# Attention keys and values stored as high and low parts by the phases that make them, and inverse sums spread by a broadcasting load

## The reference, cut to what matters

```python
q = rms_norm((x @ wq)...)      # 16 query heads of 128
k = rms_norm((x @ wk)...)      # 4 key/value heads of 128, 100 keys of x itself
v = x @ wv
k_ctx, v_ctx = rms_norm(h_ctx_kv @ wk_ctx), h_ctx_kv @ wv_ctx     # 722 keys of the context
q, k = rotary(q), rotary(k)
k_full, v_full = concat([k_ctx, k]), concat([v_ctx, v])           # 822 keys per batch
probs = softmax(q @ k_full.T * scale + mask)      # the mask is causal over the last 100 keys
out = (probs @ v_full) @ wo
```

## Time and profile before

| | |
|---|---|
| Median of 3 runs | 2796.28 us (2796.06 to 2798.22) |
| Profiled execution, its own time | 2798.06 us |
| Span of the profiled execution | 2796.0 us |
| Mean granted TensorE clock | 0.994 of full speed |
| PE busy | 2751.0 us, 98% of the span |
| DVE busy | 1586.5 us, 57% |
| ACT busy | 1104.9 us, 40% |
| Moved by DMA | 203.43 MB, 73 GB/s |
| Attention, 1445 to 1850 us: PE, DVE, ACT busy | 399.62, 345.32, 311.50 us of 405.00 |

### The profile page before, as it was taken

How to read it: one execution, slowest core, us unless ns; L and a number is a source line. 1 busy time by engine, 2 the same in 40 slices (tenths; PEclk the granted TensorE clock), 3 DMA queues, 4 the chain that set the end, 5 groups by cost and what they waited for, 6 DMA issues and landing times.

```text
span 2796.0 us, 39798 instructions
## 1 busy us (share of the span) xinstructions
PE 2751.0 (98%) x15494; PEld 2506.0 (90%) x15494; DVE 1586.5 (57%) x2106; ACT 1104.9 (40%) x1718; POOL 28.8 (1%) x45
## 2 busy tenths in 40 slices
PE   8999999999999999999999999999999999999997
PEld 7888889888888888898878888889999999998997
DVE  3223322344544454557778888854984573672767
ACT  3333322332323222334457777742542241341432
POOL 0000000000000000000000000000000000000000
PEclk9999999999999999999999999999999999999999
DMA  5222233221111111204122222212211121121222
GB/s 181 85 85 85 90 99 99 89 72 46 60 45 60 45 60 46 74 32 93 60 66 67 69 70 68 71 37 90 91 61 63 58 76 63 67 71 57 76 76 107
DMA packets 88137, 203.43 MB, mean 73 GB/s; under 512 B 9476, under 2 KB 64260, under 8 KB 73832
## 3 DMA queue, kind: packets, MB, share of 16 engines
q1 hardware_dynamic: 88040, 202.09, 21.7%
HBM read 171.86 MB, written 30.21 MB: 72 GB/s over the span
## 4 chain that ended last, share of the span: by engine, by line
PE 95%; DVE 3%; ACT 1%; issue 0%; DMA 0%; DVEq 0%; POOL 0%; SPq 0%; ACTq 0%
PE PS L128 8%; PE PS L130 8%; PE PS L129 8%; PE PS L2011 5%; PE PS L2009 5%; PE PS L2013 5%; PE PS L1533 5%; PE PS L434 3%; PE PS L435 3%; PE PS L436 3%; PE PS L409 3%; PE PS L410 3%; PE PS L411 3%; PE PS L1546 3%; PE PS L2046 3%; PE PS L2045 2%
## 5 line engine op out<-in xcount | busy, mean ns | idle before, releaser
L128 PE MATMUL PS<-XH,WH 128*128 128x512 f32 (+1 forms) x1216 | 424.5, 349 | 0.5 <-DVE t_ROOM L2281 0.5
L130 PE MATMUL PS<-XH,WL 128*128 128x512 f32 (+1 forms) x1216 | 419.7, 345 | 0.0
L129 PE MATMUL PS<-XL,WH 128*128 128x512 f32 (+1 forms) x1088 | 373.6, 343 | 0.0
L88 ACT ACTIVATE WH<-RAW 128x1024 fp32r<-128x1024 f32 x106 | 112.2, 1059 | 461.5 <-PE PS L130 329.6
L94 DVE TENSOR_TENSOR WL<-RAW,WH 128x1024 fp32r<-128x1024 f32 x106 | 129.6, 1223 | 244.8 <-ACT WH L88 244.2
L130 PEld LDWEIGHTS PS<-XH,WL 128*128 128x128 f32 x1216 | 228.8, 188 | 25.7
L128 PEld LDWEIGHTS PS<-XH,WH 128*128 128x128 f32 x1216 | 228.7, 188 | 24.9 <-ACT G L764 1.4
L129 PEld LDWEIGHTS PS<-XL,WH 128*128 128x128 f32 x1088 | 204.5, 188 | 23.0
L2137 ACT ACTIVATE WH<-RAW 128x512 fp32r<-128x512 f32 x180 | 113.5, 631 | 226.4 <-PE PS L2013 120.7
L409 PE MATMUL PS<-CH,KWH 128*128 128x338 f32 (+1 forms) x512 | 167.9, 328 | 12.9 <-DVE CL L385 12.9
L2370 DVE TENSOR_TENSOR WL<-RAW,WH 128x512 fp32r<-128x512 f32 x196 | 134.6, 687 | 60.5 <-ACT WH L2137 57.1
(11 more groups left out here) (316 smaller groups left out, 6577.8 us busy)
## 6 DMA issues: line engine op xcount, KB each, us to landing
RAW<-weights_dram SPq DMA_DIRECT2D x111, 1024.0 KB, 4.8
a_KRAW<-keys_scratch SPq DMA_DIRECT2D x32, 411.0 KB, 3.1
a_VRAW<-values_scratch SPq DMA_DIRECT2D x32, 384.0 KB
R<-context_dram SPq DMA_DIRECT2D x8, 1352.0 KB, 6.9
R<-context_dram SPq DMA_DIRECT2D x7, 1536.0 KB, 7.0
values_scratch<-VS SPq DMA_DIRECT2D x40, 256.0 KB
keys_scratch<-KS SPq DMA_DIRECT2D x8, 768.0 KB, 6.3
keys_scratch<-KS SPq DMA_DIRECT2D x8, 676.0 KB, 5.9
```

Source lines behind the costliest of these rows:

```text
L128: pe.matmul(out, wh, xh[:, k, cols], start=(k == 0), stop=False)
L129: pe.matmul(out, wh, xl[:, k, cols], start=False, stop=False)
L130: mm = pe.matmul(out, wl, xh[:, k, cols], start=False, stop=(k == KT - 1))
```

## The change

- The context phase writes the keys as a high part (ACT, `key_hi`) and a low part (DVE, `key_low`) into `KS`, one copy for both halves, and the values as a high part (ACT, `value_hi`) and a low part (DVE, a subtraction in place of the copy) into two tiles, the second of which lies in slot 0 of `RAW`. `kscr` and `vscr` have both parts, so each store becomes two.
- For that reason the weight stream of the retention phase waits until all value stores have landed.
- The heads phase does the same for the 100 keys and values of `x`. The first two values get their high parts (`value_hi`) on ACT after the loop over the kept values, the others and the keys in turns 0 and 1. The parts of the keys lie in parts of `QX` that the values or later heads use, so ACT waits before `key_hi(2)` until all 16 value stores have landed, and DVE waits in turn 1, head 0, before `finish`, until the four stores of keys 0 and 1 have landed.
- The attention phase loads the parts straight into the tiles that PE reads; the two ACT and the two DVE instructions are gone. Four small ACT instructions clear the padding once.
- The inverse sums are stored from `INV` to 1600 bytes of DRAM, and then loaded to all 128 partitions by one broadcasting load. The diagonal on POOL, the float32 matmul on PE and the copy on ACT are gone. The order in `SPREAD` is token, head in place of head, token.

```diff
@@ context
-        KS = sb("KS", [P, 2, KV_N, CA])
+        KS = sb("KS", [P, 2, KV_N, CA], F32R)
-        VS = sb("VS", [P, 3, KV_N * HD])
+        VS = [sb("VS", [P, 3, KV_N * HD], F32R)[:],
+              c.RAW[:, 0, 0:3 * KV_N * HD].bitcast(F32R).rearrange("p (t n) -> p t n", t=3)]
 store(b, e):
-                sp.wait_ge(k_out, 4 * (2 * b + e) + 4 + 4)
+                sp.wait_ge(k_lo, 4 * (2 * b + e) + 4 + 2)
+                for part in range(2):
+                    ... kscr[ds(b, 1), :, :, part, offset[e]:offset[e] + w] <- KS[:, part, :, 0:w]
                 sp.wait_ge(v_out, 6 * b + 3 * e + 3 + 2)
                 for t in range(3):
+                    for part in range(2):
+                        ... vscr[ds(b, 1), :, 0:rows, part, 3 * e + t, :] <- VS[part][0:rows, t, :]
 scalar, body:
+                    def key_hi(h):
+                        act.wait_ge(k_out, 8 * b + (n0 + h + 5))
+                        if h == 0:
+                            act.wait_ge(k_stored, 64 * b + (32 * e + 16))
+                        act.activation(KS[:, 0, h, 0:w], RS[:, h % 2, 0:w], ACT.Copy).then_inc(k_hi, 1)
+                    def value_hi(t):
+                        act.wait_ge(v_raw, 6 * b + (n + 1))
+                        if t == 0:
+                            act.wait_ge(v_stored, 192 * b + (96 * e + 16))
+                        act.activation(VS[0][0:rows, t, :], c.PS[0:rows, 4 + n % 2, :],
+                                       ACT.Copy).then_inc(v_hi, 1)
                     for h in range(KV_N):
+                        if h == 2:
+                            value_hi(0)
                         ...
-                        act.wait_ge(k_out, 8 * b + (n0 + h + 3))
+                        act.wait_ge(k_lo, 8 * b + (n0 + h + 1))
                         rsqrt_from(...)
+                        if h == 1:
+                            key_hi(0); key_hi(1); value_hi(1)
+                    key_hi(2); key_hi(3); value_hi(2)
 vector, body:
-                        dve.tensor_copy(VS[0:rows, t, :], ...).then_inc(v_out, 1)
+                        dve.wait_ge(v_hi, 6 * b + (n + 1))
+                        dve.tensor_tensor(VS[1][0:rows, t, :], c.PS[...], VS[0]..., ALU.subtract)
                     key_out(0)
                     key_out(1)
                     x_low(range(4, 6))
+                    key_low(0)
+                    key_low(1)
                     value_out(1)
                     x_low(range(6, 8))
                     key_out(2)
                     key_out(3)
+                    key_low(2)
+                    key_low(3)
                     value_out(2)
@@ retention, sync
             sp.dma_start(DECAY[:], c.decay).then_inc(c.const_in, 16)
             sp.dma_start(GNW[:], c.gnw).then_inc(c.const_in, 16)
+            sp.wait_ge(before.v_stored, 16 + 192 * B)
             weight_stream(c, sp, U_RET // 2 + 2, 2 * RH)
@@ heads
 sync:
             for v in range(KV_N):
                 sp.wait_ge(v_copied, v + 1)
+                for part in range(2):
                     for lo, hi, chunk, row in (...):
                         ... vscr[:, v, row:row + hi - lo, part, chunk, :] <- VT[part][lo:hi, v]
+            store_key(0)     # waits for k_lo, then two DMAs of 128 partitions
+            store_key(1)
             weight_stream(c, sp, U_V // 2 + 6, 1)
-            for v in range(KV_N): (store key v)
+            store_key(2)
+            store_key(3)
             weight_stream(c, sp, U_V // 2 + 8, 3)
 scalar:
             act.activation(ONE[:], c.ONES_HD[:], ACT.Copy)
+            value_hi(0)
+            value_hi(1)
+            def key_hi(v):
+                act.wait_ge(out, 2 + v + 1)
+                if v == 2:
+                    act.wait_ge(v_stored, 16 * V_STORES)
+                act.activation(key_parts(v)[0], key_raw(v), ACT.Copy).then_inc(k_hi, 1)
 scalar, turn, after SQH:
+                    if first and j < 2:  value_hi(j + 2)
+                    if first and j >= 2: key_hi(j - 2)
+                    if i is 1 and j < 2: key_hi(j + 2)
                     root(...)
 vector:
             copy_value(0)          # now waits for value_hi(0) and subtracts
             split_lo(c, dve, U_V + 4)
             copy_value(1)
             split_lo(c, dve, U_V + 5)
 vector, turn, after square_lo:
+                    if first and j < 2:  copy_value(j + 2)
+                    if first and j >= 2: key_low(j - 2)
+                    if i is 1 and j < 2:
+                        key_low(j + 2)
+                        if j == 0:
+                            dve.wait_ge(k_stored[0], 64)
                     finish(...)
+            after turn 1: dve.wait_ge(v_stored, 256); dve.wait_ge(k_stored[1], 64)
-            before turn 3: dve.wait_ge(stored, 16 * KV_STORES)
@@ attention
 sync, for each stage:
+                    sp.wait_ge(inverted, 4 * b + (v + 1))
+                    sp.dma_start(c.iscr, INV[:, v % 2, :]).then_inc(inverse_out, 16)
                     load_keys(next but one)      # now two DMAs, high and low
+                    sp.wait_ge(inverse_out, 64 * b + (16 * v + 16))
+                    sp.wait_ge(o_out, 4 * b + (v + 1))
+                    sp.dma_start(SPREAD[:], c.iscr.rearrange("(a t) g -> a (t g)", a=1)
+                             .broadcast_to([P, GT])).then_inc(spread, 16)
                     load_values(next)            # now four DMAs
 tensor:
-                    spread_inverse(b, v)         # between scores 1 of the next head and turn 2
 scalar:
-            keys_hi, values_hi, spread_out
 vector:
-            keys_lo, values_lo
 gpsimd:
-            diagonal(b, v)
```

More of the change, by code:

```diff
@@ new lines, in sync @@
+            store_key(2)
+            store_key(3)
+            weight_stream(c, sp, U_V // 2 + 8, 3)
+            sp.wait_ge(v_stored, 16 * V_STORES)
+            sp.wait_ge(k_stored[0], 64)
+            sp.wait_ge(k_stored[1], 64)
+            sp.wait_ge(before.k_stored, 16 + 64 * B)
+            sp.wait_ge(before.v_stored, 16 + 192 * B)
+            for part in range(2):
+                sp.dma_start(c.KHL0[:, part, 0:KEYS].bitcast(F32),
+                             c.kscr[0, 0, :, part, :]).then_inc(c.k_in, 16)
@@ L1278, in turn @@
                     act.activation(SQH[:], SQ[:], ACT.Copy).then_inc(sq_hi, 1)
+                    if first and j < 2:
+                        value_hi(j + 2)
+                    if first and j >= 2:
+                        key_hi(j - 2)
+                    if i is 1 and j < 2:
+                        key_hi(j + 2)
                     if final:
@@ L1284, in scalar @@
             turn(0, True)
-            with act.Fori(1, TURNS - 1) as i:
+            turn(1, False)
+            with act.Fori(2, TURNS - 1) as i:
                 turn(i, False)
@@ L1351, in turn @@
                         square_lo(j, i)
+                    if first and j < 2:
+                        copy_value(j + 2)
+                    if first and j >= 2:
+                        key_low(j - 2)
+                    if i is 1 and j < 2:
+                        key_low(j + 2)
+                        if j == 0:
+                            dve.wait_ge(k_stored[0], 64)
                     if first and j == 0:
@@ L1406, in phase_attention @@
         RING = 4
-        KHL = room(2, KEYS_E)
+        key_room = room(KEYS_E)
+        KHL = [(c.KHL0[:, part, :], key_room[part]) for part in range(2)]
         VHL = room(2, KC * HD)
@@ L1492, in sync, with load_keys @@
-        def sync(sp, heads_done):
-            def load_keys(b, v):
-                sp.wait_ge(k_lo, 4 * b + v)
-                sp.dma_start(KRAW[:, 0:KEYS], c.kscr[ds(b, 1), v].rearrange("a p t -> (a p) t")
-                             ).then_inc(k_in, 16)
+        def sync(sp, heads_done):
+            def load_keys(b, v, first=False):
+                if not first:
+                    sp.wait_ge(s_raw, 16 * b + (4 * v - 4))
+                for part in range(2):
+                    sp.dma_start(KHL[part][v % 2][:, 0:KEYS].bitcast(F32),
+                                 c.kscr[ds(b, 1), v, :, part, :].rearrange("a p t -> (a p) t")
+                                 ).then_inc(k_in[v % 2], 16)
@@ L1672, in ahead @@
                             exponentials(*nxt, j)
-                    if second is not None:
-                        keys_hi(act, *second)
                     turned_hi(b, v, 0)
@@ L1749, in body @@
                     turned_lo(b, v, 2)
-                    if second is not None:
-                        keys_lo(dve, *second)
                     turned_lo(b, v, 3)
@@ L2617, in _ @@
                 tail[0](pool)
-                attention[1](pool, heads[-1])
                 tail[1](pool)
@@ L2625, in _ @@
                 heads[1](sp)
-                attention[2](sp, heads[-1])
+                attention[1](sp, heads[-1])
                 tail[2](sp)
@@ L2633, in _ @@
                 heads[2](act, attention[-1].first_high)
-                attention[3](act, heads[-1])
```

(5 more changed lines are left out.)

253 lines of the change are left out of this document (119 added, 134 removed).

## The result

The changed kernel takes 2824.45 us (median of 4 runs, 2823.61 to 2825.0), the kernel before 2796.84 us (median of 4, 2796.06 to 2798.22): a ratio of 1.0098, 95% interval 1.008 to 1.0115, so 27.6 us slower.

The account below looks back on a forecast made before the run. PE was taken to bound the kernel, holding 95% of the chain that ended last. Costs of 40.9 us against 24.5 us of gain made it 16.4 us slower: 2812.7 us, range 2797 to 2829 (8 in 10).

Parts of the forecast that it names:

- the restarts: After three new PE stalls the clock is granted at the lower level: 1.7 us lost each, 5.1 us cost (0 to 15).
- The end of the context: At unit 10, `GNW` lands late behind SP's doubled, later stores and PE waits: 8.7 us cost (3 to 12).
- The heads' start: PE's first heads unit waits for `value_hi(0)` on ACT, then DVE's low part and split: 4.8 us cost (4 to 6).
- turn 1: Heads phase: PE's variance waits behind 16 value stores, key stores and DVE's work: 21.3 us cost (12.2 to 25).
- context inside: In context second halves, `value_hi(0)` on ACT delays PE's fourth key variance, 0.15 us in each of 8: 1 us cost (0 to 2).
- gain of the attention phase: Attention: the spreading matmul's 0.74 us goes in 31 stages, plus both ends: 24.5 us gain (21 to 26).
- The last stage: Last attention stage: the 0.52 us wait for the diagonal and ACT's copy of about 0.5 us go: 1.0 us gain.
- That the stores land before anyone asks: Rival at ACT's wait before `key_hi(2)`: stores land in time, 23.0 us fall away, 2789.7 us; chance 0.09.
- That only the value stores count: Rival in turn 1 of the heads: keys land early, 9.1 us less, 2803.6 us; chance 0.14.
- The lower clock for longer: Rival on PE's clock after the new stalls: three restarts at about 6 us in place of 1.7, 2826 us; chance 0.08.
- The pair of DMAs late for `output`: Rival in the attention stages: inverse sums arrive late, PE waits 1 us a stage, 32 us, 2845 us; chance 0.05.
- The held ACT in the context: Rival at the context's `value_hi(0)`: the doubled 82-row store holds ACT 7 times about 3 us, 2834 us; chance 0.04.

Follow-up runs that it names:

- the constants' experiment: The changed kernel with the loads DECAY and GNW put on SP's queue ahead of the last context half's six value stores: 2814.86 us.
- The experiment with the roots first: The changed kernel with ACT's roots of keys 0 and 1, then the value copy, ahead of the chunk split in a context half: 2816.58 us.
- the cut stores: The changed kernel with the heads phase's value stores cut by rows (46 into 32 and 14, 54 into 48 and 6): 2799.44 us.
- the four edits: The changed kernel with roots ahead of the chunk split, constants ahead of the last value stores, early value copy in the heads, and cut value stores: 2771.32 us.
- the keys' other place: The changed kernel with the parts of keys 2 and 3 kept where nothing is waiting to be stored: 2825.39 us.
- the last experiment: The kernel before with the spreading load (key and value loads first on SP's queue) and roots ahead of the context's chunk split, without stored parts: 2777.8 us.

## Why the prediction was right in sign and too small

**Right.** The mechanism held in the places that decide the sign. The losses outside the attention phase (41 us forecast with the restarts, 48.2 us measured up to the last awaited variance of the heads) outweigh its gain. The end of the context was forecast at 8.7 us and cost 9.2, its wait 8.0 and 8.44, `GNW` being late behind SP's doubled value stores; that this was the cause is shown by the constants' experiment. The heads' start was 4.8 and is 4.67. In turn 1, 21.3 was said and 22.9 came, by the path that was said: value stores, key stores behind them, `finish`, 7.1 us of DVE's work (7.3 measured; the text adds 1331.5 and 7.1 to 1338.8, which is 0.2 us too much). The two parts of a store do share what carries them, as was assumed: 16 stores hold SP for 44.36 us, twice the 22.62 us of 8. The key stores took 1356.40 - 1340.35 = 16 us from first issue to landing. The restarts came to 6.5 us against 5.1, 1.7 to 2.8 us each where 1.7 was said. The spreading load was hidden: it lands 5.8 us after its issue (7.4 us after that of the store ahead of it, 1610.39 to 1612.01 + 5.8, where 7.2 was said), and DVE's output waits for PE's last weighing alone, 31 times.

**Wrong, the term "context inside".** It was sized at 1.0 us (0 to 2) and is 5.5. The step was: the copy takes 0.6 us, the logarithm had been done 0.44 us before PE's fourth variance, so 0.15 us in each of 8 second halves. Both numbers of it were a little off, and the count was. The copy takes 0.60 us, but the logarithm of key 1 starts 6.11 us behind the first variance where it started 5.43 us behind (347.19 and 343.77): 0.68 us later. And of the 0.44 us only 0.29 were cover: in the changed kernel the logarithm ends at 347.19 + 0.53 = 347.72 and PE, which waits for it, starts at 347.87, so 0.15 us is what the release takes. That makes 0.68 - 0.29 = 0.39 us, the measured difference of the gaps (0.70 and 0.31). The first halves, which the prediction left out, lose 0.21 us in the same gap (0.56 us from 314.22 to 314.78, before 0.35 from 311.77 to 312.12), and the matmul that has waited takes 0.26 and 0.23 us to the next one, where it took 0.17 and 0.16. That is 0.39 + 0.21 + 0.09 + 0.07 = 0.76 us, the whole difference of a batch, 67.83 us against 67.07. The experiment with the roots first shows the cause.

**Too large, the term "gain of the attention phase".** Forecast 24.5 us (21 to 26), measured 22.1. The 30 stages between the first output and the last but one were forecast at 0.74 us each and give 0.67, 20.2 us. In the stage, the eight transposes behind the removed matmul take 0.71 us to the next matmul, where they took 0.62:

```profile
1612.19 0.93 PE L1633 MATMUL PS<-ID,a_E 100*128 100x100 f32 x8
1612.90 0.43 PE L1647 MATMUL PS<-XH 128*128 128x400 f32 x1
```

```profile
1611.46 1.05 DVE L1777 TENSOR_TENSOR XL<-PS,XH 128x400 fp32r<-128x400 f32 x2
```

The second four of these transposes need the second of DVE's two low parts, which ends at 1611.46 + 1.05 = 1612.51; PE comes to them at about that time. The matmul had covered this: 0.74 us went and a wait of some 0.09 us came in its place. In a full stage that semaphore is read off the times, since the view shows no idle time inside a group. In the last stage, where no scores lie between, the same two turns show the wait with its label:

```profile
1865.80 1.24 PE L1633 MATMUL PS<-ID,a_E 100*128 100x100 f32 x8 [0.86 <-DVE XL L1777]
```

No run tried it by itself; that a stage gives 0.59 to 0.69 us and not 0.74, all ten kernels show in which the spreading load holds nothing. The prediction had looked for the tightest link at the turn's first transposes, behind the last exponential; it was at the fourth turn, behind DVE. The last stage was forecast at 1.0 us of gain. It gives none to speak of, since that wait of 0.86 us stands where the diagonal's wait of 0.52 us and the matmul had been: from its first transposes to the first matmul of the tail PE takes 10.72 us (1864.04 to 1874.76) against 10.95 us (1838.10 to 1849.05). The beginning was forecast at 0.6 us ahead of the first score and 0.74 us for the first stage, and gave 0.8 and 1.8 us; in that first stage both kernels have stretches at the lower clock, so the 1.8 us are not the matmul's alone.

**The rivals.** That the stores land before anyone asks (2789.7) is refuted for the change as it stood, by the 44.36 us; the cut stores made it true (2799.4), and the four edits together go beyond it, to 2771.3. That only the value stores count (2803.6) is refuted by the keys' other place: without the wait for value stores turn 1 waits as long. The lower clock for longer (2826) has nearly the measured time and is refuted all the same, the restarts being 6.5 us and not 18; a time that fits is no cause shown. The pair of DMAs late for `output` (2845) was not seen in any stage. The held ACT in the context (2834) named the right engine at a wrong place: not the 82-row store held it, but its own extra copy.

## What to carry to other kernels

Moving work into an earlier phase moves its stores too, and on an in-order queue the price is paid by whoever stands behind them: here 16 stores of 46 and 54 rows cost 25 us and a two-line constant load 9.6 us, for 4 to 5 us of gain, while the part of the change that needed none of it (the broadcasting load) was worth 18 us alone. Look at how a store's row count divides before doubling it (46 rows cut into 32 and 14 took 26 us off the queue here), and put small loads with a known due time ahead of bulk stores. And when a cover is a few tenths of a microsecond in a loop, work out both instructions' starts from one common event before calling the cost nothing.

## What the runs showed of the hardware

- A DMA that few engines carry holds the queue that issues it: at a DMA share of 0.14, SP needed 288 ns for the fastest and 5,651 ns for the slowest of the 16 value stores, and 24 better cut ones took 18.30 us together against 44.36. `DECAY`, a load of its own data, took 4.20 us to issue behind the context's last stores and 1.08 us when it was put ahead of them.
- DVE's output took 869 ns where it had taken 568, for the same 128x400 elements, once it read the inverse sums four elements apart (token by head) in place of side by side. The tile is also written by a DMA now and no longer by ACT; no run parts the two. It was hidden: no row shows an instruction that waited for it.
- After PE's idle 8.44, 4.67 and 22.90 us its clock was granted at the lower level (1.2 GHz) for 5.2, 3.3 and 4.4 us of its work, which cost 2.6, 1.7 and 2.2 us beyond the wait, not in the order of the waits' lengths. After an idle time of 2.32 us (548.12 in the kernel before) it fell too; after one of 2.30 us (570.99 in the last experiment) it did not.
